# First tiles' halves in another order, and the split of a chunk shared anew between two engines

## The reference

```python
# layer 0: feed-forward with a conditioned RMS norm and a quantized down projection
scale = cond @ norm_w.T + 1.0
h = x * (scale[:, None, :] * rsqrt(mean(x * x) + 1e-6))
val, gate = split(h @ up_w.T)                 # 2 x 1024 wide
h = val * gelu(gate)
x = act_quant(h) @ weight_quant(down_w).T + x # 8 bit rows, ternary weights
# layer 1: an adapter whose weights are made from the condition
Wd_b = Wd + ((cond @ Wdd.T + bdd) * 0.1).reshape(B, 128, 256)
Wu_b = Wu + ((cond @ Wdu.T + bdu) * 0.1).reshape(B, 256, 128)
x = x + relu(x @ Wd_b.T + bd) @ Wu_b.T + bu
```

## Time and profile before

| | |
|---|---|
| median of 3 runs | 480.48 us (479.61 to 481.18) |
| profiled execution | 480.89 us |
| its span in the profile | 479.2 us |
| TensorE (PE) busy | 467.1 us, 97% |
| VectorE (DVE) busy | 377.8 us, 79% |
| ScalarE (ACT) busy | 365.5 us, 76% |
| GpSimd (POOL) busy | 260.2 us, 54% |

### The profile page before, as it was taken

One profiled execution on the slowest core, in us unless ns is written; L12 is line 12 of the kernel. 1 busy time (PEld: TensorE's weight loads), 2 busy tenths in 40 slices (PEclk: granted clock), 3 DMA queues, 4 the chain that ended last, 5 costly groups with the idle time before them and its releaser, 6 DMA issues.

```text
span 479.2 us, 10039 instructions
## 1 busy us (share of the span) xinstructions
PE 467.1 (97%) x3278; PEld 271.3 (57%) x3278; DVE 377.8 (79%) x789; ACT 365.5 (76%) x636; POOL 260.2 (54%) x676
## 2 busy tenths in 40 slices
PE   8989999999999999999999999999999999999995
PEld 7445656666565455555555555555555555555563
DVE  4798988898898787877877788786777877777776
ACT  5889999999997678768676876867776777777662
POOL 0295775657655446475573746557374543444653
PEclk9999999999999999999999999999999999999997
DMA  7957787777873455565554466455445544544332
GB/s 269 349 113 205 180 244 227 189 210 181 253 176 89 92 121 100 137 147 117 148 133 107 128 141 155 111 153 126 103 136 133 143 103 119 130 123 90 72 85 89
DMA packets 117860, 71.01 MB, mean 148 GB/s; under 512 B 102000, under 2 KB 102960, under 8 KB 115632
## 3 DMA queue, kind: packets, MB, share of 16 engines
q1 hardware_dynamic: 117648, 70.29, 57.2%
q10 hardware_dynamic: 160, 0.07, 0.1%
HBM read 37.44 MB, written 8.39 MB: 96 GB/s over the span
## 4 chain that ended last, share of the span: by engine, by line
PE 88%; DVE 5%; ACT 3%; issue 2%; DMA 1%; POOL 0%; DVEq 0%; ACTq 0%; SPq 0%; POOLq 0%
PE bank L1022 64%; PE bank L1036 11%; PE bank L1113 4%; PE bank L1127 4%; PE bank L1095 4%; PE bank L993 1%; DVE adapt L716 1%; ACT gel L552 1%; DVE xs_lo L746 1%; DMA qT<-qn 1%; DVE hid L767 1%; DVE amax L775 1%; ACT tern L650 0%; ACT qn L574 0%; DVE x L879 0%
## 5 line engine op out<-in xcount | busy, mean ns | idle before, releaser
L767 DVE SCALAR_TENSOR_TENSOR hid<-bank,rms,gel 128x512 f32<-128x512 f32 x127 | 95.2, 750 | 80.4 <-ACT gel L552 79.4
L552 ACT ACTIVATE gel<-bank,rms 128x512 f32<-128x512 f32 x127 | 86.9, 684 | 90.7 <-PE bank L1022 90.6
L1022 PE MATMUL bank<-up_hi,xs_hi 128*128 128x512 f16 x508 | 151.2, 379 | 3.0 <-DVE hid L767 1.5
L1022 PE MATMUL bank<-up_lo,xs_hi 128*128 128x512 f16 x508 | 151.1, 379 | 0.7 <-DVE up_lo L931 0.7
L1022 PE MATMUL bank<-up_hi,xs_lo 128*128 128x512 f16 x508 | 151.1, 379 | 0.0
L1022 PEld LDWEIGHTS bank<-up_lo,xs_hi 128*128 128x128 f16 x508 | 49.6, 98 | 60.9 <-DVE up_lo L931 1.4
L1022 PEld LDWEIGHTS bank<-up_hi,xs_lo 128*128 128x128 f16 x508 | 49.7, 98 | 59.9
L775 DVE TENSOR_REDUCE amax<-hid 128x1 f32<-128x1024 f32 x63 | 76.9, 1220 | 2.2
L565 ACT ACTIVATE hid<-hid,amax 128x1024 f32<-128x1024 f32 x64 | 72.4, 1132 | 2.3 <-DVE amax L781 1.8
L403 POOL TENSOR_TENSOR wsplit<-stage,wsplit 128x288 f16<-128x288 f32 x64 | 52.8, 853 | 34.9 <-ACT wsplit L527 34.9
L1022 PEld LDWEIGHTS bank<-up_hi,xs_hi 128*128 128x128 f16 x508 | 48.3, 98 | 38.5 <-DVE xs_lo L746 2.9
(11 more groups left out here) (129 smaller groups left out, 633.3 us busy)
## 6 DMA issues: line engine op xcount, KB each, us to landing
xT_s<-in_xT SPq DMA_DIRECT2D x32, 256.0 KB, 3.0
xn_s<-in_xn SPq DMA_DIRECT2D x32, 256.0 KB, 3.1
stage<-in_WddT SPq DMA_DIRECT2D x8, 1024.0 KB, 5.4
stage<-in_WduT SPq DMA_DIRECT2D x8, 1024.0 KB, 5.2
out<-out_s SPq DMA_DIRECT2D x31, 256.0 KB, 2.4
...
qT<-qn SPq DMA_TRANSPOSE x63, 3.1
```

Source lines behind the costliest of these rows:

```text
L552: nc.scalar.activation(gel[:, c], u_gate[c][:], ACT.Gelu, scale=rms[:, t // TPB % XN_SLOTS, t % TPB:t % TPB + 1]).then_inc(gelu_done, 1)
L767: nc.vector.scalar_tensor_tensor(out=hid[:, t % 2, c * 512:(c + 1) * 512], in0=u_val[c][:], scalar=rms[:, t // TPB % XN_SLOTS, t % TPB:t % ...
L1022: ins = nc.tensor.matmul(dst[:], a[:, t // TPB % 2, k, cols], w[:, c, k, v, :], start=(k == 0 and n == 0), stop=(k == KD - 1 and n == 2))
```

## The change

**Steps 0 to 3 by hand.** On ScalarE, VectorE, GpSimd and TensorE the first steps are taken out of the loop and written out. TensorE does the first halves of tiles 0 and 1 together and then the second halves (`up_first`), with all passes that need only the high half of the weights first, and the passes with `up_lo` behind them; tile 1 gets banks of its own for this (`u_banks`). The idle matmuls are 6 and 4 instead of 8 and 9. VectorE makes `xs_hi` of the first sequence and does the root behind the `up_lo` operations. The down weights are loaded and summed in two parts; the sum's matmuls stand in step 3, the ternary operations in steps 3 and 4 on VectorE. `down(0)` stands in step 4, `down(1)` and `down(2)` in step 5, and from step 6 on it is `down(s - 3)` again. Order on SP: an up piece comes first, then `xT` of sequence 0, the other pieces, `xn`; base weights ahead of chunk 0, sequence 3 behind chunk 1.

**Chunks two steps later, and split in another way.** Chunk `q` is handled in step `4 + q` instead of `2 + q`, and `generate(q)` in `5 + q`; the first adapter comes in step 23 instead of 21, with 24 slots for `x1` instead of 20. `high_part` is one operation over the whole chunk; VectorE scales the 1,152 columns in place before its `low_part`, and GpSimd waits for that scaling.

**Order of passes.** `up` does the pass with `xs_lo` last, and waits for it only there.

**The end.** `q_transpose` ahead of `down(62)`, `middle(B-2)` between two transposes, `total(B-4)` ahead of VectorE's evacuation, and GpSimd's output biases in another order: the last pieces wait until VectorE's last subtractions are done.

```diff
-IDLE_FIRST = 8
-IDLE_SECOND = 9
+IDLE_FIRST = 6
+IDLE_SECOND = 4
+FIRST = 4
+CHUNK_STEP = [FIRST + q for q in range(NGEN)]
 def adapter_step(b):
-    return max(2 * b + 7, NGEN + 5 + (4 * b + 2) // 3)
+    return max(2 * b + 7, CHUNK_STEP[-1] + 4 + (4 * b + 2) // 3)
...
+def downs(s, c):
+    late = {(4, 1): [0], (5, 0): [1], (5, 1): [2]}
+    return late.get((s, c), [s - DOWN] if c == 0 and s - DOWN >= 3 else [])
+def residuals(s):
+    return {4: [0], 5: [1]}.get(s, [s - DOWN] if s - DOWN >= 3 else [])
...
+            for n in range(NC * KD):
+                sp.dma_start(raw_up[:, n // KD, n % KD], up_wT[:, n // KD, n % KD]).then_inc(ld_up[n], 16)
+                if n == 0:
+                    sp.dma_start(xT_s[:, 0], xT[0]).then_inc(ld_xT[0], 16)
...
             def high_part(q):
-                first, rest = slice(CHUNK - POOL_COLS, CHUNK), slice(0, CHUNK - POOL_COLS)
-                nc.scalar.activation(stage[:, q % 2, first], stage[:, q % 2, first], ACT.Copy, scale=W_SCALE
-                                     ).then_inc(w_scaled, 1)
-                nc.scalar.activation(wsplit[:, q % 2, 0, rest], stage[:, q % 2, rest], ACT.Copy, scale=W_SCALE
-                                     ).then_inc(w_hi_v, 1)
-                act.wait_ge(w_scaled, q + 1)
-                nc.scalar.copy(wsplit[:, q % 2, 0, first], stage[:, q % 2, first]).then_inc(w_hi_p, 1)
+                nc.scalar.activation(wsplit[:, q % 2, 0], stage[:, q % 2], ACT.Copy, scale=W_SCALE).then_inc(w_hi, 1)
...
             def low_part(q):
-                dve.wait_ge(w_hi_v, q + 1)
+                dve.wait_ge(w_hi, q + 1)
+                first = slice(CHUNK - POOL_COLS, CHUNK)
+                nc.vector.tensor_scalar(stage[:, q % 2, first], stage[:, q % 2, first], W_SCALE, None, ALU.mult
+                                        ).then_inc(w_scaled, 1)
...
             def up(t, c):
-                    passes = ((xs_hi, up_hi), (xs_lo, up_hi), (xs_hi, up_lo))
+                    passes = ((xs_hi, up_hi), (xs_hi, up_lo), (xs_lo, up_hi))
...
+            gelu(2, 0)
+            quantize(0)
+            quantized(0)
+            gelu(2, 1)
+            absolute_sum(1)
+            scaled_high(2)
+            gelu(3, 0)
+            quantize(1)
+            quantized(1)
+            gelu(3, 1)
+            quantize(2)
+            quantized(2)
+            squares(3)
```

More of the change, by code:

```diff
@@ L61 @@
 AM_SLOTS = 8
-X1_SLOTS = 20
+X1_SLOTS = 24
 X1N_SLOTS = 4
@@ L933, in _ @@
                                                ).then_inc(up_ready, 1)
-            for s in range(NT):
+            rsqrt_guess(0)
+            rsqrt_first()
+            scaled_low(1)
+            rsqrt_guess(1)
+            gate(0, 0)
+            gate(0, 1)
+            gate(1, 0)
+            quant_scale(0)
+            gate(1, 1)
+            gate(2, 0)
+            rsqrt_guess(2)
+            quant_scale(1)
+            gate(2, 1)
+            split_cond()
+            quant_scale(2)
+            gate(3, 0)
+            scaled_low(2)
+            ternary_first()
+            gate(3, 1)
+            ternary_second()
+            ternary_third()
+            for s in range(FIRST, NT):
                 if s == LAST_T:
@@ L1169, in _ @@
                     up_last(1)
-                if s == 1:
-                    pe.wait_ge(absum_ready, 1)
-                    nc.tensor.matmul(sum_ps, ones[:], wsum[:, 0:1], start=True, stop=True).then_inc(absum_full, 1)
+                for t in downs(s, 1):
+                    down(t)
                 for q in chunk(s, 1):
```

258 lines of the change are left out of this document (152 added, 106 removed).

## The result

The changed kernel takes **484.04 us** (482.85 to 484.26, 4 runs) against 480.24 (479.61 to 481.18, 4 runs): ratio 1.0062, 95% interval 1.0044 to 1.0080. It is slower by 0.6%, where a gain to 476.7 was forecast, and it lies outside the range of 473.6 to 479.9. The profiled execution took 482.85, with a span of 481.1 us. Of all executions in this document one, of `e11_passes0_end`, was in the chip's slow state (541.64 us) and is left out.

A forecast was written before the change was run, and what follows sets the result against it. TensorE, busy 467.1 of 479.2 us, was taken as the bound, so only its 12 us of waits could be won. 480.89 + 0.9 - 2.0 - 2.7 = 477.1, as a median 476.7; range 473.6 to 479.9.

The forecast's parts named there:

- Head: Steps up to tile 8: TensorE starts 2.9 us earlier but waits eat it; 0.9 slower, range -1.5 to +2.5.
- the wait of 1.6 for the second piece: Head: TensorE waits 1.6 us behind its first 4 matmuls until up_hi of the second up piece is ready.
- The walked waits: Head, TensorE: 1.1 and 1.5 us at tiles 3 and 5, 0.8 and 0.6 at tile 4, 0.1 at down(0), 1.7 plus 0.2 at down(2).
- Chunk steps: Steps with a chunk: waits for xs_lo go, VectorE becomes the bound by 0.2 us a pair; -2.0, ends -2.3 and +1.3.
- some 1.3 of slack: Chunk steps: the new order of passes and GpSimd's late need give 1.3 us, used up by 7 pairs at 0.2.
- The scaling's own size: Chunk steps: VectorE's added operation on 1,152 fp32 columns takes 0.7 us, with 0.6 and 0.95 as ends.
- Tail: The end of the kernel: transposes, subtractions, middle(B-2), totals and biases reordered; -2.7 us, from -1.2 to -3.3.
- the forecast's -3.3: Tail: the far end, -3.3 us, if TensorE's lower clock after 460 us stays away.
- the swap: Tail: q_transpose ahead of down(62), so its evacuations lie beside the down; 0.3 us gained.
- subtractions, totals and biases: Tail: output_bias no longer beside the x1n subtractions, 0.8 us; one total less and last bias off the last subtractions, 0.9.
- From execution to median: Whole kernel: the profiled execution lies 0.4 us above the median, so 477.1 becomes 476.7.
- The contended scaling: Rival, chunk steps: VectorE's scaling or low_part runs against GpSimd, VectorE sets the pace; 487.7 us, half of it 482; chance 0.08.

The follow-up runs named there:

- e11_passes0_end: The kernel before with the change's end and its order of passes for all tiles but tile 0; 475.29 us.
- e6: The kernel before with only the change's order of passes (the pass with xs_lo last, waited for only there); 480.63 us.
- e19: The changed kernel with VectorE's scaling and low part of a chunk moved ahead of two small operations of quant_scale; 481.34 us.
- e14: The changed kernel with the old three-operation ScalarE split, GpSimd released by ScalarE, plus VectorE's scaling written to the side; 489.08 us.

## Why the prediction was wrong

In its own terms, for the profiled execution (forecast 477.1, measured 482.85):

- **Head, forecast +0.9.** (Its own figures, 67.6 against 66.8, give 0.8.) At tile 8 the changed kernel stands at 67.97 + 2.8 = 70.8 against 66.8: **+4.0**, beyond the end of 2.5 that I gave it. The start failed: 8.39 instead of 6.9, tile 2 at 20.4 instead of 18.9, 1.5 us. I had moved `norm_w`'s matmuls forward by two idle ones (4.05) without asking when its load lands behind the new order of loads (6.75), and had no term for a lowered clock. From the first matmul to tile 2 it is 12.0, as forecast, but by luck: the wait of 1.6 for the second piece isn't in the rows, and the lowered clock stands in its place. The walked waits were found at the forecast places and a little short: 6.0 forecast behind the two tiles, 6.2 in the rows and about 1 more by how the trace ends a matmul; for GpSimd 0.2 was forecast and 0.94 came. From tile 2 to tile 8 it took 1.6 more than forecast (47.5 for 45.9), and 1.1 of that goes with the old split (tile 2 to the end of the third `generate` is 47.5 and 46.4).
- **Chunk steps, forecast -2.0.** Measured +1.6 from tile 8 on, beyond the end of +1.3. The step that failed is "GpSimd's part is waited for only 7 us later. That gives some 1.3 of slack". One step later is 7.45 us, but gate, maximum, scaling and GpSimd's 3.6 fill it; the slack was 0.15, readable in the trace of before. The order of passes alone gave what I had for the whole (1.3 + 0.85 by e6's stretches); the split took 3.2 back in the 15 steps and 0.75 before them. The scaling's own size was right (0.74, start to start 0.65, for 0.7), and ScalarE's operation took 1.90 for 1.8. VectorE was not the bound: in e19, with the same load on it, most of the late pairs take 15.03 instead of 15.40.
- **Tail, forecast -2.7.** Measured -3.65, of which about 0.6 is the clock, as the forecast's -3.3 allowed. The mechanism holds. By the traces the swap with 0.9 for 0.3 and `middle(B-2)` with 1.2 for 0.65 were sized too small, and subtractions, totals and biases with 1.0 for 0.8 + 0.9 too large. The granted clock rose from 0.85 to 0.98 after 460.
- **From execution to median.** I took 0.4 off; the changed kernel's median lies 1.2 above its profiled execution. Its head starts with `norm_w`'s landing, at 6.5 to 8.0 in eleven profiles with that order of loads, and then has the clock at one level or the other: tile 2 starts at 19.2 to 23.1 in them.
- **Rivals.** The contended scaling had the nearest time (482 at half its price), with the wrong cause: low part and scaling take 1.08 and 0.74 in the changed kernel, as alone. Where they do collide its price was near: 16.7 a pair worked out, 8.14 + 8.22 = 16.4 in e14. What happened was no rival of mine.

Not settled: why `norm_w` lands up to 1.5 us later in one execution than in another, how much of the medians' distance to the profiled executions is due to it, and why e6's median shows no gain.
